# A cross-attention and graph kernel: left-out keys replaced in the context, rows transposed under the output product, reordered steps

## The chip, the cores and the metric

The kernel runs on one core of a Trainium2 chip. A core has five engines that run side by side and are tied together only by semaphores: TensorE (PE, with its weight loads as PEld), VectorE (DVE), ScalarE (ACT), GpSimd (POOL) and SyncE (SP), which here only issues DMAs. The metric is the device time of one execution in microseconds; the median over runs is compared.

## What is computed

Four layers in a row on x of shape (4, 256, 512) with a context of shape (4, 64, 512). The reference, cut to what matters:

```python
# L0: low-rank update mixed by a router
w = softmax(x @ router_W.T + router_b)
a_sum = einsum('bsh,arh->bsr', x, ctx)              # sum over the four A's
x = nan_to_num(x + 0.5 * einsum('bsn,bsnh->bsh', w, einsum('bsr,nhr->bsnh', a_sum, lora_B)))
# L1: cross-attention, 32 heads of 16, then LayerNorm
Q, K, V = x @ Wq.T + bq, ctx @ Wk.T + bk, ctx @ Wv.T + bv
attn = softmax(where(mask, Q K^T / 4, -inf)) V      # by head
x = layernorm(x + attn @ Wo.T + bo) * ln_g + ln_b
# L2 and L3, the same twice: graph of the 8 nearest, 4 blocks each
idx = the 8 nearest of 512 points, from ctx as coordinates (b, 64, 512)
for i in range(4):
    p = leaky_relu(x)
    x = (w[i] p + sum over the 8 neighbours of w[i] p) / 9 + x   # w[i] = fside[i]
```

## The kernel before

Everything runs once, batch element by batch element (b is 0 to 3), with x held transposed in four chunks of 128 features.
The order of work is written out by hand as five tables of step names, one for each engine (`PE_STEPS`, `ACT_STEPS`, `DVE_STEPS`, `POOL_STEPS`, `SP_STEPS`). A step is `kind b _ i : slot`, so `w1_2:3` is the third weights product of batch element 1, written to PSUM slot 3. There are four PSUM slots, each of 128 x 1024 fp32. Each engine walks its table strictly in order and waits on semaphores, so a step that waits holds up all that stands behind it on that engine. A slot is reused once the step that last read it is done (`wait_read` in the PE block).

The steps that matter here, by kind:

- `lora`, `router`, `mixed`, `update`: the first layer. `low` (ACT) copies the low-rank product, `rA`, `rE`, `rB` make the router's softmax and the mixture, `mh` and `ml` split it into high and low part, `raw` and `nan` (DVE) give x1.
- `dist`: distances of points, then `near` (DVE: maximum of 8 and replacement, four times for each batch element), then `adjT` on PE and `adjC` on ACT turn the marks into the adjacency matrix. `sq` (ACT) squares the coordinates as they land.
- `keys` and `values`: products of the context for all four batch elements at once. After `keys`, `kf` (ACT) adds the bias, `fm` (DVE) replaces every key that the mask leaves out by the mean of the attended keys (L989 to L999), `kh` (ACT) makes the high part, `kl` (POOL) the low part, and `kst` and `ks` (SP) carry them through HBM into `k_stack`.
- `query`: x1 times Wq in 48 matmuls; `qf`, `qh` (ACT), `ql` (POOL), then `qsh` and `qs` (SP) stack it into `q_stack`.
- `sc` and `mx`: scores for the row maximum (`shift`). `w`: the exact scores from the stacks. `ex` (ACT): the exponential. `at`: attention in 32-column tiles, with the sums of the exponentials beside it. `rc` (DVE): reciprocal of the sums. `norm`: the reciprocals are handed out to 128 rows by a product with `row_of` (L477, called from the `norm` branch). `dv`: division. `out`: product with Wo.
- `rows` (L601): x1 is transposed into a slot of its own; `ra` (ACT) copies it to `points`, `rw` (POOL) adds bo, `ad` (DVE) adds the output product and takes the statistics; `ce`, `dev`, `ln` are the LayerNorm.
- `lk`, `ph`, `pl`, `wp`, `uh`, `ul`, `sp`, `pt`: the 32 units of the graph layers (8 for each batch element). `wp` is 24 matmuls of 256 columns, `sp` is 16 of 512. `pl` on POOL makes the low part p_lo.

PE issues nearly all of its products through one helper, so L477 stands for most of them and the rows are told apart by the names of the tiles. In the rows, `slot<-xyz_n,xyz` and `slot<-points 128x512` are both `dist` (the coordinates of batch element 1 are parked in `points`), `slot<-ctx_t,wk` is `keys`, `slot<-x_hi,wq_hi` is `query`, `slot<-wv,ctx_t` is `values`.

The loads are issued by SP at the start, in this order (L377): coordinates of batch element 0, context, router weights, x of batch element 0, coordinates of 1, router bias, lora_B, Wk, mask, Wq, Wv, bv, x of 1, bo, Wo, the LayerNorm vectors, and the coordinates of 2.

## Time and profile before

| | us |
|---|---|
| median of 3 runs | 430.8 (429.2 to 431.13) |
| the profiled execution | 429.93 |
| its span, first to last instruction | 428.2 |
| PE busy | 389.0 (91% of the span) |
| DVE, ACT, POOL busy | 277.1, 156.3, 125.7 |
| mean granted clock of PE | 0.971 |

The profiled execution took 429.93 us, of which 1.7 lie outside its span; it is 0.9 below the median. The page gives sums over the whole span, then 40 slices of 10.7 us, the chain that ended last, and the costliest groups. A share of busy time is a mean over stages with different limits: the front of this kernel (the first 100 us or so) and the graph layers (from about 220 us) have to be read apart, with the timeline of each engine.

### The profile page before, as it was taken

The page shows a single profiled execution, that of the slowest core. Times are in us where ns is not written, and L with a number is a line of the kernel's source. Part 1 is how long each engine was busy: PE and PEld are TensorE (multiplying, and loading weights), DVE is VectorE, ACT ScalarE, POOL GpSimd, SP SyncE. Part 2 cuts the span into 40 slices and gives each one's busy share as a digit, 9 for nine tenths or more (in the row PEclk, how much of TensorE's full clock was granted, in tenths as well). Part 3 has the DMA queues.
Part 4 walks back from the last instruction along what each step waited for, and adds up shares of the span by engine and source line. Part 5 has one row for each costly group of instructions (what it writes and reads, how often), then busy time and mean ns, then how long its engine had stood idle before and what let it go on. Part 6 is the DMA issues. An engine that isn't in the chain of part 4 may idle for free.

```text
span 428.2 us, 5965 instructions
## 1 busy us (share of the span) xinstructions
PE 389.0 (91%) x2368; PEld 310.6 (73%) x2368; DVE 277.1 (65%) x304; ACT 156.3 (37%) x194; POOL 125.7 (29%) x78
## 2 busy tenths in 40 slices
PE   3775599869999899899999999999999999999995
PEld 1561568649659576576485998899988899888894
DVE  3824996591796767735856986567665654756543
ACT  1206405164545776233760331323323232222320
POOL 8405203220120344020324254244333341233420
PEclk9898699969999989999999999999999999999999
DMA  7980211440250353083000000000000001000012
GB/s 185 393 281 2 99 37 51 113 120 8 51 135 8 99 125 69 0 142 51 1 2 0 2 0 2 0 2 1 2 0 2 0 2 49 2 0 2 0 51 98
DMA packets 25004, 23.35 MB, mean 55 GB/s; under 512 B 8977, under 2 KB 20113, under 8 KB 24977
## 3 DMA queue, kind: packets, MB, share of 16 engines
q1 hardware_dynamic: 24528, 22.97, 19.8%
q8 instruction: 19, 0.31, 0.3%
q14 instruction: 9, 0.07, 0.1%
q10 hardware_dynamic: 448, 0.01, 0.1%
HBM read 13.26 MB, written 3.15 MB: 38 GB/s over the span
## 4 chain that ended last, share of the span: by engine, by line
PE 78%; DVE 7%; SPq 5%; ACT 4%; issue 3%; DMA 2%; ACTq 0%; DVEq 0%
PE slot L477 77%; SPq L377 5%; DMA xyz_n<-in_ctx 2%; DVE shift L1073 2%; ACT probT L805 2%; DVE k_full L989 1%; DVE near_of L981 1%; PE slot L579 1%; PE slot L587 1%; DVE top L980 1%; ACT adj L715 0%; ACT wq_hi L700 0%; DVE inv_sums L1084 0%; ACT k_full L706 0%; DVE k_part L995 0%
## 5 line engine op out<-in xcount | busy, mean ns | idle before, releaser
L894 POOL TENSOR_TENSOR p_lo<-p_full,p_hi 128x1024 fp32r<-128x1024 f32 x32 | 80.0, 2500 | 152.0 <-ACT p_hi L838 152.0
L477 PE MATMUL slot<-adj,u_hi 128*128 128x512 f32 x256 | 65.9, 399 | 0.1
L477 PE MATMUL slot<-adj,u_lo 128*128 128x512 f32 x256 | 64.8, 395 | 0.0
L1147 DVE SCALAR_TENSOR_TENSOR points<-slot,points 128x1024 f32<-128x1024 f32 x32 | 39.2, 1224 | 38.9 <-PE slot L477 38.9
L1141 DVE TENSOR_TENSOR u_lo<-slot,u_hi 128x1024 fp32r<-128x1024 f32 x32 | 39.2, 1224 | 34.4 <-ACT u_hi L847 34.4
L838 ACT ACTIVATE p_hi<-p_full 128x1024 fp32r<-128x1024 f32 x32 | 33.7, 1054 | 70.3 <-DVE p_full L1136 70.2
L847 ACT ACTIVATE u_hi<-slot 128x1024 fp32r<-128x1024 f32 x32 | 32.8, 1026 | 69.8 <-PE slot L477 69.8
L477 PEld LDWEIGHTS slot<-adj,u_lo 128*128 128x128 f32 x256 | 48.3, 188 | 11.2
L1136 DVE SCALAR_TENSOR_TENSOR p_full<-points 128x1024 f32<-128x1024 f32 x32 | 53.4, 1670 | 3.3 <-DVE points L1147 0.5
L477 PEld LDWEIGHTS slot<-adj,u_hi 128*128 128x128 f32 x256 | 47.2, 189 | 11.2 <-issue 1.0
L477 PE MATMUL slot<-fs_hi,p_hi 128*128 128x256 f32 x256 | 52.4, 286 | 0.0
L477 PE MATMUL slot<-fs_lo,p_hi 128*128 128x256 f32 x256 | 51.5, 283 | 0.0
L477 PE MATMUL slot<-fs_hi,p_lo 128*128 128x256 f32 x256 | 51.4, 282 | 0.0
L477 PEld LDWEIGHTS slot<-fs_hi,p_hi 128*128 128x128 f32 x256 | 40.7, 190 | 3.2 <-issue 1.3
L477 PEld LDWEIGHTS slot<-fs_lo,p_hi 128*128 128x128 f32 x256 | 39.7, 191 | 0.0
L477 PEld LDWEIGHTS slot<-fs_hi,p_lo 128*128 128x128 f32 x256 | 39.7, 191 | 0.0
L477 PE MATMUL slot<-wo,attT 128*128 128x512 f32 x64 | 28.2, 593 | 0.2 <-DVE attT L1088 0.2
L911 POOL TENSOR_TENSOR adj<-adj,ident 128x512 fp32r<-128x512 f32 x4 | 6.2, 1561 | 56.1 <-ACT adj L715 56.1
L477 PEld LDWEIGHTS slot<-wo,attT 128*128 128x128 f32 x64 | 12.0, 190 | 13.9 <-issue 13.4
L805 ACT ACTIVATE probT<-slot,mask_col 128x1024 f32<-128x1024 f32 x16 | 17.6, 1112 | 11.1 <-PE slot L477 11.1
L1042 DVE SCALAR_TENSOR_TENSOR x_in<-slot,x_in 128x1024 f32<-128x1024 f32 x4 | 4.9, 1222 | 23.4 <-PE slot L477 23.4
L917 POOL TENSOR_TENSOR points<-points,bo_all 128x1024 f32<-128x1024 f32 x4 | 9.5, 2376 | 34.9 <-ACT points L745 34.9
(136 smaller groups left out, 547.8 us busy)
## 6 DMA issues: line engine op xcount, KB each, us to landing
q_stack<-q_hi SPq DMA_DIRECT2D x32, 128.0 KB, 2.4
x_in<-in_xT SPq DMA_DIRECT2D x4, 512.0 KB, 5.1
q_stack<-q_lo SPq DMA_DIRECT2D x16, 128.0 KB, 3.1
out_points<-points SPq DMA_DIRECT2D x4, 512.0 KB, 2.8
loraB_raw<-in_lora_BT SPq DMA_DIRECT2D x1, 1024.0 KB, 7.9
wk<-in_WkT SPq DMA_DIRECT2D x1, 1024.0 KB, 10.1
wq_raw<-in_WqT SPq DMA_DIRECT2D x1, 1024.0 KB, 11.8
wv<-in_WvT SPq DMA_DIRECT2D x1, 1024.0 KB, 14.0
```

Of the source, the lines that this page charges most:

```text
L377: sp.dma_start(dst, src).then_inc(loads[name], 16)
L477: return pe.matmul(dst, lhsT, rhs, start=start, stop=stop, skip_group_check=True)
L805: act.activation(probT[:, i % 2, :], psum[slot_of["w", b, i]][:], ACT.Exp, bias=mask_col[:, b:b + 1], scale=QK_SCALE).then_inc(prob_ready, 1)
L838: act.activation(p_hi[b][:], p_full[:, nth["lk", b, i] % 2, :], ACT.Copy).then_inc(p_hi_ready, 1)
L847: act.activation(u_hi[:, n % 2].rearrange("p m o -> p (m o)"), psum[slot_of["wp", b, i]][:], ACT.Copy).then_inc(u_hi_ready, 1)
L894: pool.tensor_tensor(lo, full, hi.bitcast(F32), ALU.subtract).then_inc(ready, 1)
L911: pool.tensor_tensor(own, own.bitcast(F32), ident[:].unsqueeze(1).broadcast_to([P, KC, P]), ALU.add)\
L917: pool.tensor_tensor(pts, pts, bo_all[:].unsqueeze(1).broadcast_to([P, ST, H]), ALU.add)\
L1073: dve.tensor_reduce(pairs, psum[slot_of["sc", b, i]][:].rearrange("p (j a v) -> p j a v", a=2, v=V), AX_X, ALU.max, negate=True).then_inc( ...
L1136: dve.scalar_tensor_tensor(p_full[:, n % 2, :], pts, SLOPE, pts, ALU.mult, ALU.max)\
L1141: dve.tensor_tensor(u_lo[:, n % 2].rearrange("p m o -> p (m o)"), psum[slot_of["wp", b, i]][:], u_hi[:, n % 2].rearrange("p m o -> p (m o) ...
L1147: dve.scalar_tensor_tensor(pts, psum[slot_of["sp", b, i]][:], 1.0 / (TOPK + 1), pts, ALU.mult, ALU.add).then_inc(points_ready, 1)
```

## The change

- **Left-out keys.** The replacement is made before the product with Wk: `fm` masks the context into `ctx_m`, takes the mean of the attended context vectors and copies it over the left-out ones. `keys` then reads `ctx_m`. `kf` is gone; `kh` makes the high part straight from PSUM with the bias; `kl` moves from POOL to DVE and reads PSUM.
- **Rows under the output product.** `xb` (ACT) adds bo to x1 while it is still transposed and writes `x_bo`; `rows` transposes that into the slot in which `out` then accumulates. `ra`, `rw` and the addition in `ad` are gone; `st` takes the statistics, and `ce` its input, from PSUM. The slot is held from `rows` to `ce`.
- **Sums by two row tiles.** The order of heads inside `w` and `at` is rotated so that the sums of one feature chunk lie in one block of partitions. `norm` then contracts over 64 partitions instead of 128, the four products alternate between the upper and the lower half of the array, and two that follow each other write different PSUM banks.
- **Smaller edits.** The router's maximum is subtracted inside the exponential (one DVE operation fewer), the weights are normalized in the product that makes the mixture, `qh` reads PSUM instead of the SBUF copy, POOL's subtractions are cut in two or four pieces, and three of POOL's clears become steps of its table.
- **Orders.** All five tables are written anew, and so is the order of the loads: context, x of 0, mask, coordinates of 0, lora_B, Wk, coordinates of 1, x of 1, the bias columns, Wq, bo as a column (4 bytes for each descriptor), Wv, bv, the mask's columns, Wo, the LayerNorm vectors, the coordinates of 2. Router weights and bias go through ACT's queue.

The diff, cut to its core (of each table only the first line):

```diff
--- before.py
+++ after.py
...
 PE_STEPS = """
-dist0_0:0 lora0:1 dist0_1:2 router0:3 adjT0:1 keys:0 mixed0:2 lora1:3 dist1_0:1 router1:0 dist1_1:3 update0:2
...
+lora0:0 dist0_0:1 router0:2 dist0_1:3 keys:0 lora1:1 mixed0:3 values:2 router1:0 update0:1 adjT0:3 mixed1:2
...
     slot_of = {step[:3]: step[3][0] for step in pe_steps if step[3]}
+    slot_of.update({("out", b, 0): slot_of["rows", b, 0] for b in range(B)})
...
+            load(ctx_t[:], chunks(ctxT), "ctxT")
+            load_x(0)
+            load(mask_all_i[:], mask.rearrange("b v -> (b v)").unsqueeze(0).broadcast_to([P, B * V]), "mask_all")
             load_xyz(0)
-            load(ctx_t[:], chunks(ctxT), "ctxT")
-            load(a_router[:, :, R:R + NE], chunks(router_WT), "routerW")
-            load_x(0)
-            load_xyz(1)
-            load(rb_all[:], router_b.unsqueeze(0).broadcast_to([P, NE]), "rb")
             load(loraB_raw[:], chunks(lora_BT), "loraB")
             load(wk[:], chunks(WkT), "wk")
-            load(mask_all_i[:], mask.rearrange("b v -> (b v)").unsqueeze(0).broadcast_to([P, B * V]), "mask_all")
+            load_xyz(1)
+            load_x(1)
+            load(bk_col[:], bk_cols, "bk")
+            load(bq_col[:], bq_cols, "bq")
             load(wq_raw[:], chunks(WqT), "wq")
+            sp.dma_start(bo_col[:], bo.rearrange("(c p) -> p c", p=P), allow_slow_non_contiguous=True)\
+                .then_inc(loads["bo_col"], 16)
             load(wv[:], chunks(WvT), "wv")
             load(bv_all, bv.unsqueeze(0).broadcast_to([P, H]), "bv")
-            load_x(1)
-            load(bo_all[:], bo.unsqueeze(0).broadcast_to([P, H]), "bo")
+            for half in range(2):
...
+                load(mask_col_i[half * V:(half + 1) * V, :], maskT, "mask_col")
...
-                    loaded(pe, "ctxT")
+                    pe.wait_ge(ctx_filled, 1)
                     for c in range(KC):
                         for k in range(KC):
-                            last = mm(ps[:, c * B * V:(c + 1) * B * V], wk[:, k, c * P:(c + 1) * P], ctx_t[:, k, :],
+                            last = mm(ps[:, c * B * V:(c + 1) * B * V], wk[:, k, c * P:(c + 1) * P], ctx_m[:, k, :],
...
-                    after(pe, x1_ready, "nan", b)
+                    pe.wait_ge(idents, 1)
+                    after(pe, x_bo_ready, "xb", b, each=KC)
                     for t in range(ST):
                         for k in range(KC):
-                            last = pe.transpose(ps[:, t * H + k * P:t * H + (k + 1) * P],
-                                                x1[:, k, t * P:(t + 1) * P], ident[:])
-                    last.then_inc(rows_done, 1)
+                            pe.matmul(ps[:, t * H + k * P:t * H + (k + 1) * P], x_bo[b][:, k, t * P:(t + 1) * P],
+                                      ident[:], start=k == 0, stop=False, is_transpose=True, skip_group_check=True)
...
-                        pair = 4 * i + j
+                        pair = 4 * ((j + i) % KC) + j
...
-                        mm(ps[PART * j:PART * (j + 1), i * S:(i + 1) * S], v_blk[:, 4 * i + j, :],
+                        c = (j + i) % KC
+                        mm(ps[PART * j:PART * (j + 1), c * S:(c + 1) * S], v_blk[:, 4 * c + j, :],
                            probT[:, i % 2, j * S:(j + 1) * S], True, True)
                     for j in range(4):
-                        last = mm(sums[PART * j:PART * (j + 1), 0:S], sum_cols[:, i, :],
+                        c = (j + i) % KC
+                        last = mm(sums[PART * c:PART * (c + 1), 0:S], sum_cols[:, j, :],
                                   probT[:, i % 2, j * S:(j + 1) * S], i == 0, i == KC - 1)
                     last.then_inc(attend_done, 1)
                 elif kind == "norm":
-                    pe.wait_ge(blk_consts, 3)
+                    pe.wait_ge(rows_set, 1)
                     after(pe, inv_ready, "rc", b)
-                    for c in range(KC):
-                        last = mm(ps[:, c * S:(c + 1) * S], row_of[:, c, :], inv_sums[:], True, True)
+                    for c in (0, 2, 1, 3):
+                        rows = slice(2 * PART * (c // 2), 2 * PART * (c // 2 + 1))
+                        last = mm(ps[:, c * S:(c + 1) * S], row_of[rows, c % 2, :], inv_sums[rows, :], True, True)
...
-                                      k == 0, k == KC - 1)
+                                      False, k == KC - 1)
...
-                elif kind == "kf":
+                elif kind == "kh":
                     loaded(act, "bk")
                     act.wait_ge(keys_done, 1)
                     ps = psum[slot_of["keys", 0, 0]]
                     for c in range(KC):
-                        act.activation(k_full[:, c, :], ps[:, c * B * V:(c + 1) * B * V], ACT.Identity,
-                                       bias=bk_col[:, c:c + 1]).then_inc(k_ready, 1)
-                elif kind == "kh":
-                    act.wait_ge(k_filled, 1)
-                    act.activation(kT_hi[:], k_full[:], ACT.Copy).then_inc(k_hi_ready, 1)
+                        act.activation(kT_hi[:, c, :], ps[:, c * B * V:(c + 1) * B * V], ACT.Identity,
+                                       bias=bk_col[:, c:c + 1]).then_inc(k_hi_ready, 1)
...
-                elif kind == "ra":
-                    after(act, rows_done, "rows", b)
+                elif kind == "xb":
+
+                    loaded(act, "bo_col")
+                    after(act, x1_ready, "nan", b)
                     if b == 1:
-                        act.wait_ge(k_stored, 32)
+                        after(act, dist_done, "dist", 1, 1)
                     if b == 2:
                         act.wait_ge(v_ready, 1)
-                    act.activation(points[:, b].rearrange("p t n -> p (t n)"), psum[slot_of["rows", b, 0]][:],
-                                   ACT.Copy).then_inc(row_copied, 1)
+                    for c in range(KC):
+                        act.activation(x_bo[b][:, c], x1[:, c, :], ACT.Identity, bias=bo_col[:, c:c + 1])\
+                           .then_inc(x_bo_ready, 1)
...
-            def low_part(lo, full, hi, ready):
-                pool.tensor_tensor(lo, full, hi.bitcast(F32), ALU.subtract).then_inc(ready, 1)
+            def low_part(lo, full, hi, parts, ready):
+
+                n = lo.shape[1] // parts
+                for k in range(parts):
+                    cut = slice(k * n, (k + 1) * n)
+                    pool.tensor_tensor(lo[:, cut], full[:, cut], hi[:, cut].bitcast(F32), ALU.subtract)\
+                        .then_inc(ready, 1)
...
+                    link(dve.tensor_tensor(ctx_m[:], ctx_t[:],
                                            attended[:].unsqueeze(1).broadcast_to([P, KC, B * V]), ALU.mult))
-                    link(dve.tensor_reduce(k_sum[:], k_full[:].rearrange("p c (b v) -> p c b v", b=B), AX_X, ALU.add))
-                    link(dve.tensor_tensor(k_mean[:], k_sum[:], per_count[:].unsqueeze(1).broadcast_to([P, KC, B]),
+                    link(dve.tensor_reduce(ctx_sum[:], ctx_m[:].rearrange("p c (b v) -> p c b v", b=B), AX_X, ALU.add))
+                    link(dve.tensor_tensor(ctx_mean[:], ctx_sum[:], per_count[:].unsqueeze(1).broadcast_to([P, KC, B]),
                                            ALU.mult))
+                    dve.copy_predicated(ctx_m[:].rearrange("p c (b v) -> p c b v", b=B),
+                                        left_out[:].bitcast(U32).rearrange("p (b v) -> p b v", b=B).unsqueeze(1)
+                                        .broadcast_to([P, KC, B, V]),
+                                        ctx_mean[:].unsqueeze(3).broadcast_to([P, KC, B, V])).then_inc(ctx_filled, 1)
+                elif kind == "kl":
+                    dve.wait_ge(ctx_filled, 1)
+                    ps = psum[slot_of["keys", 0, 0]]
                     for c in range(KC):
-                        last = dve.tensor_tensor(k_part[:, c].rearrange("p (b v) -> p b v", b=B),
-                                                 left_out[:].rearrange("p (b v) -> p b v", b=B),
-                                                 k_mean[:, c].unsqueeze(2).broadcast_to([P, B, V]), ALU.mult)
-                    link(last)
-                    dve.tensor_tensor(k_full[:], k_full[:], k_part[:], ALU.add).then_inc(k_filled, 1)
+                        dve.wait_ge(k_hi_ready, 2 * (c // 2 + 1))
+                        dve.scalar_tensor_tensor(kT_lo[:, c, :], ps[:, c * B * V:(c + 1) * B * V], bk_col[:, c:c + 1],
+                                                 kT_hi[:, c, :].bitcast(F32), ALU.add, ALU.subtract)\
+                           .then_inc(k_lo_ready, 1)
...
-                elif kind == "ad":
-                    after(dve, row_ready, "rw", b)
-                    ps = psum[slot_of["out", b, 0]]
+                elif kind == "st":
+                    ps = psum[slot_of["rows", b, 0]]
                     for t in range(ST):
                         after(dve, half_output if t == 0 else output_done, "out", b)
-                        pts = points[:, b, t]
-                        dve.tensor_tensor(pts, pts, ps[:, t * H:(t + 1) * H], ALU.add).then_inc(sum_ready, 1)
-                        dve.wait_ge(sum_ready, ST * nth["ad", b, 0] + t + 1)
-                        link(dve.bn_stats(stats[:, b, t], pts))
...
+                        link(dve.bn_stats(stats[:, b, t], ps[:, t * H:(t + 1) * H]))
...
-                        dve.scalar_tensor_tensor(points[:, b, t], points[:, b, t], mean_var[:, b, t, 0:1], g_all[:],
-                                                 ALU.subtract, ALU.mult).then_inc(centered, 1)
+                        dve.scalar_tensor_tensor(points[:, b, t], ps[:, t * H:(t + 1) * H], mean_var[:, b, t, 0:1],
+                                                 g_all[:], ALU.subtract, ALU.mult).then_inc(centered, 1)
```

How the orders move. TensorE at the start, before:

```order
L477 MATMUL slot<-xyz_n,xyz 128x512 x2
L477 MATMUL slot<-x_in,points 72x256 x4
L477 MATMUL slot<-xyz_n,xyz 128x512 x2
L561 MATMUL slot<-ident,low 128x72 x2
L579 MATMUL slot<-ident_h,near_of 128x128 x16
L477 MATMUL slot<-ctx_t,wk 128x256 x16
L587 MATMUL slot<-ident,mix 128x128 x8
L477 MATMUL slot<-x_in,points 72x256 x4
L477 MATMUL slot<-points 128x512 x2
L561 MATMUL slot<-ident,low 128x72 x2
L477 MATMUL slot<-points 128x512 x2
```

and with the change (`slot<-ctx_m,wk` is `keys`):

```order
L480 MATMUL slot<-x_in,points 72x256 x4
L480 MATMUL slot<-xyz_n,xyz 128x512 x2
L566 MATMUL slot<-ident,low 128x72 x2
L480 MATMUL slot<-xyz_n,xyz 128x512 x2
L480 MATMUL slot<-ctx_m,wk 128x256 x16
L480 MATMUL slot<-x_in,points 72x256 x4
L592 MATMUL slot<-ident,mix 128x128 x8
L480 MATMUL slot<-wv,ctx_t 128x512 x8
L566 MATMUL slot<-ident,low 128x72 x2
L480 MATMUL slot<-mixT_hi,loraB_hi 128x256 x4
L480 MATMUL slot<-mixT_hi,loraB_lo 128x256 x4
L480 MATMUL slot<-mixT_lo,loraB_hi 128x256 x4
```

`lora` of batch element 0 now opens; `keys`, the second `lora` and `values` stand ahead of the first `adjT` (the 16 transposes of `near_of`) and of both `dist` products of batch element 1.

ScalarE at the start, before (`xyz_n<-xyz_n` is `sq` of batch element 2, `adj<-slot` is `adjC`):

```order
L697 ACTIVATE loraB_hi<-loraB_raw 128x2048
L726 ACTIVATE lge<-lgs 128x16
L694 ACTIVATE xyz_n<-xyz_n 64x512
L715 ACTIVATE adj<-slot,taken_bias 128x2048
L700 ACTIVATE wq_hi<-wq_raw 128x2048
L706 ACTIVATE k_full<-slot,bk_col 128x256 x4
L732 ACTIVATE mixT_hi<-slot 128x1024
L723 ACTIVATE low<-slot 72x256
L710 ACTIVATE kT_hi<-k_full 128x1024
```

and with the change (`points<-points` is `sq` of batch element 1):

```order
L703 ACTIVATE loraB_hi<-loraB_raw 128x2048
L730 ACTIVATE lge<-lg,small 128x8 x2
L700 ACTIVATE points<-points 64x512
L706 ACTIVATE wq_hi<-wq_raw 128x2048
L712 ACTIVATE kT_hi<-slot,bk_col 128x256 x4
L788 ACTIVATE k_blk_hi<-kT_hi,half_col 32x4x64 x8
L736 ACTIVATE mixT_hi<-slot 128x1024
L726 ACTIVATE low<-slot 72x256
L700 ACTIVATE xyz_n<-xyz_n 64x512
```

`sq` of batch element 2 stood ahead of `adjC`, `mh` and the second `low`, and stands behind `kh`, `kb`, `mh` and that `low` now.

VectorE around the keys, before:

```order
L987 RECIPROCAL per_count<-count 128x4
L989 TENSOR_TENSOR k_full<-k_full,attended 128x1024
L991 TENSOR_REDUCE k_sum<-k_full 128x16
L992 TENSOR_TENSOR k_mean<-k_sum,per_count 128x16
L995 TENSOR_TENSOR k_part<-left_out,k_mean 128x256 x4
L999 TENSOR_TENSOR k_full<-k_full,k_part 128x1024
L1037 TENSOR_TENSOR mixT_lo<-slot,mixT_hi 128x1024
```

and with the change, first the part ahead of the product, then the part behind it:

```order
L1010 TENSOR_TENSOR ctx_m<-ctx_t,attended 128x1024
L1012 TENSOR_REDUCE ctx_sum<-ctx_m 128x16
L1013 TENSOR_TENSOR ctx_mean<-ctx_sum,per_count 128x16
L1015 COPY_PREDICATED ctx_m<-left_out,ctx_mean 128x1024
L1046 TENSOR_TENSOR lg<-slot,rb_all 128x16
```

and

```order
L1054 SCALAR_TENSOR_TENSOR mix<-slot,small,lge 128x512 x2
L984 TENSOR_SCALAR mask_col<-mask_col_i 128x4
L1024 SCALAR_TENSOR_TENSOR kT_lo<-slot,bk_col,kT_hi 128x256 x4
L1060 TENSOR_TENSOR mixT_lo<-slot,mixT_hi 128x1024
L1030 TENSOR_TENSOR v_rows<-slot,points 128x1024
```

The mask arithmetic of eight operations that stood between the product and the first `ml` is now ahead of the product and of the first router step; behind the product four operations on a quarter of the columns each are left.

## Rows read from the trace of the kernel before

**Rows 1.** The page: busy time of the engines, and GB/s in 40 slices of 10.7 us.
```profile
PE 389.0 (91%) x2368; PEld 310.6 (73%) x2368; DVE 277.1 (65%) x304; ACT 156.3 (37%) x194; POOL 125.7 (29%) x78
...
GB/s 185 393 281 2 99 37 51 113 120 8 51 135 8 99 125 69 0 142 51 1 2 0 2 0 2 0 2 1 2 0 2 0 2 49 2 0 2 0 51 98
```

**Rows 2.** Waits of PE over the whole span: total us, times, longest.
```profile
PE slot L477 <- ACT xyz_n L694: 6.4, 1, 6.4
PE slot L477 <- DVE mixT_lo L1037: 6.1, 1, 6.1
PE slot L477 <- ACT adj L715: 5.5, 1, 5.5
PE slot L477 <- ACT probT L805: 4.1, 8, 1.5
PE slot L477 <- DVE shift L1073: 3.7, 1, 3.7
PE slot L579 <- DVE near_of L981: 2.9, 1, 2.9
...
PE slot L561 <- ACT low L723: 1.1, 1, 1.1
```

**Rows 3.** Windows: length, then busy us of PE, PEld, DVE, ACT, POOL, then clock, DMA share, GB/s.
```profile
0.00:63.90 63.90, 41.52 (x181) 27.90 (x182) 41.56 (x68) 17.27 (x26) 21.66 (x35) 0.89 0.52 167
63.90:100.00 36.10, 29.74 (x184) 24.08 (x182) 26.12 (x38) 16.20 (x27) 8.93 (x4) 0.91 0.32 86
100.00:230.00 130.00, 124.00 (x863) 88.75 (x862) 87.58 (x105) 66.55 (x86) 29.22 (x12) 0.99 0.27 56
230.00:428.20 198.20, 193.71 (x1147) 169.81 (x1145) 121.86 (x95) 56.28 (x56) 65.86 (x27) 1.00 0.03 11
```

**Rows 4.** Timeline of ACT: start us, us, line, operation, [idle before, releaser].
```profile
32.28 0.63 ACT L694 ACTIVATE xyz_n<-xyz_n 64x512 f32<-64x512 f32 x1 [10.56 <-DMA xyz_n<-in_ctx]
...
38.02 1.05 ACT L732 ACTIVATE mixT_hi<-slot 128x1024 fp32r<-128x1024 f32 x1
...
47.76 3.69 ACT L775 ACTIVATE k_blk_hi<-kT_hi,half_col 32x256 fp32r<-32x256 f32 x8
```

**Rows 5.** Timeline of DVE, same columns: the masking of the keys begins and ends.
```profile
38.26 4.11 DVE L989 TENSOR_TENSOR k_full<-k_full,attended 128x1024 f32<-128x1024 f32 x1 [13.34 <-ACT k_full L706]
42.40 1.22 DVE L991 TENSOR_REDUCE k_sum<-k_full 128x16 f32<-128x1024 f32 x1
...
46.47 1.22 DVE L1037 TENSOR_TENSOR mixT_lo<-slot,mixT_hi 128x1024 fp32r<-128x1024 f32 x1
```

**Rows 6.** Timeline of PE: keys, two distance steps, and the first rows step.
```profile
18.70 8.12 PE L477 MATMUL slot<-ctx_t,wk 128*128 128x256 f32 x32
...
34.95 3.37 PE L477 MATMUL slot<-points 128*128 128x512 f32 x4 [5.53 <-ACT adj L715]
...
39.69 1.96 PE L477 MATMUL slot<-points 128*128 128x512 f32 x4
...
63.86 1.04 PE L601 MATMUL slot<-ident,x 128*128 128x128 f32 x8
```

**Rows 7.** Timeline of PE: two products in 32-column tiles, then the full-array norm product.
```profile
109.57 0.64 PE L477 MATMUL slot<-probT,v_blk 128*32 128x256 f32 x8
110.03 0.61 PE L477 MATMUL slot<-probT,sum_cols 128*32 128x256 f32 x8
...
118.22 1.97 PE L477 MATMUL slot<-inv_sums,row_of 128*128 128x256 f32 x8
```

**Rows 8.** Timeline of POOL where DVE shows a long operation.
```profile
36.77 4.51 POOL L894 TENSOR_TENSOR wq_lo<-wq_raw,wq_hi 128x2048 fp32r<-128x2048 f32 x1 [0.53 <-ACT wq_hi L700]
```

**Rows 9.** DMA issues by line: KB each, median us from issue to landing.
```profile
x_in<-in_xT SPq DMA_DIRECT2D x4, 512.0 KB, 5.1
...
ctx_t<-in_ctxT SPq DMA_DIRECT2D x1, 512.0 KB, 4.4
```

**Rows 10.** Timeline of SyncE: the stack reload of the third batch element begins.
```profile
151.49 5.67 SPq L411 DMA_DIRECT2D q_stack<-q_hi  x8
```

281 lines of the change are left out of this document (143 added, 138 removed).

## The prediction, made before the change was run

> **What bounds the kernel now.** I read the page's busy times first, then what PE waits for, then the span in four windows, then the timelines of the front. PE is busy 389.0 of 428.2 us [rows 1], so at most 39.2 us of idle time are there to win besides faster work. The windows say where they lie [rows 3]. From 230 us to the end PE is busy 193.7 of 198.2 us at full clock, and the missing 4.5 us are the last update of the points and the last store, which nothing in the change shortens. From 100 to 230 us it is idle 6.0 us, mostly in eight short waits for the exponential [rows 2, 3]. From 63.9 to 100 us it is idle 6.4 us, of which 3.7 are a wait for the row maxima on DVE [rows 2, 3]. The first 63.9 us hold the rest: PE is busy 41.5 us there and idle 22.4 us, and its granted clock is 0.89 on average [rows 3]. So the graph layers are bound by PE, and the front by what PE waits for.
>
> The timelines name the chain of the front. ACT walks its table in order, and the square of the third coordinate set stood waiting 10.6 us for its load, until 32.3 us [rows 4]. Behind it stood the adjacency copy (5.5 us of PE's waits) and the high part of the first mixture, at 38.0 us [rows 2, 4]. Then DVE spent 38.3 to 46.5 us on the masked keys before it came to the low part of that mixture, for which PE waited 6.1 us [rows 2, 5]. The first of those mask operations took 4.11 us, where the next one of the same width took 1.22; it ended at 42.37, and POOL's subtraction beside it ended at 36.77 + 4.51 = 41.28 [rows 5, 8]. The other waits before 63.9 us are 6.4 us for the first coordinates, 2.9 for the neighbours and 1.1 for the low-rank copy [rows 2].
>
> **Term 1, the front's waits.** I follow the new order with durations of the rows.
>
> - Start. The context is now issued first and x second, at about 0.8 and 1.4 us by the issue times of the old first loads. With 4.4 and 5.1 us to landing [rows 9] they are there at 5.2 and 6.5, and the sum over the context on DVE needs 1.3 us behind the first. I let the first product start at 7.5, against 6.4 before: 1.1 us lost.
> - Keys. The product needs Wk and the masked context. Through Wk 3.5 MB are issued; at 185 GB/s in the first 10.7 us and 393 GB/s after it [rows 1] that is 2.0 MB and then 1.5 MB in 3.9 us, so 14.6 us. The mask chain took 46.47 - 38.26 = 8.2 us [rows 5]. Without the hold-up beside POOL (4.11 - 1.22 = 2.9) and with one predicated copy in place of five operations (a gain of about 1.3) it is 4.0. It starts behind about 2.6 us of small operations from 6.5 on, so it ends at 13.1, or at 15 if POOL's clears hold it up once. Keys start near 15 instead of 18.7 [rows 6]. PE has two distance steps, a router and a low-rank product to do till then, and hardly waits.
> - From there PE has the second low-rank product, the mixture, values and a router step, some 10 us of work behind the 7 of keys, so until 32. The first low part of the mixture needs the new ACT chain: keys end at 22, then 1.6 for the high part, 3.7 for the block of keys (it took 3.69 [rows 4]), 1.05 and 1.22 for the two parts of the mixture [rows 4, 5]: 29.6. So it comes 2.4 us ahead of its use, and the 6.1 us wait is gone. The square of the third coordinates still waits to about 32 us, but what stands behind it is wanted later than that. The 5.5 us and the 1.1 us waits go too.
>
> What is late next is the second mixture's low part, behind the first x1 on DVE: I get about 1 us of wait. PE's idle time in this stage falls from 22.4 to 7.5 + 0.5 to 1, say 8.0: **14.4 us won**. At best 15.4, with no later wait; at worst 10, if keys start no earlier than at 18.7 as before.
>
> **Term 2, the clock of the front.** At a clock of 0.89 over 63.9 us, 11% is lost, which is 14 us at the half level of 1.2 GHz. About half of it lies under idle time. A distance step at 34.95 us took 3.37 us, just behind the 5.5 us wait, and the next 1.96 [rows 6]; keys took 8.12 us. Without the long waits most of this goes; the first steps at the very start stay slow. I take **4.5 us**, with 0 and 7 as ends.
>
> **Term 3, the sums handed out by two row tiles.** One norm step takes 1.97 us [rows 7]. The trace of before has no row tiles, but it has column tiles: four 256-column products in four 32-column tiles start at 109.57, and the next four at 110.03, so 0.46 us for four, against 1.97 for four on the full array [rows 7]. Two tiles at a time should take half: 0.98. Four steps win 4 x 0.98 = 3.9; at worst nothing, if the halves run one after the other. I take **3.8**.
>
> The page on tiling (the Trainium skill, TensorEngine Tiling, section Tiling Modes) says that a change of the tiling mode drains the array. By it each norm step would pay for two changes of mode and give part of the 3.8 us back. The trace shows no such price: the 32-column products at 109.57 and 110.03 follow each other and their neighbours without a gap beyond 0.1 us [rows 7], so the sum keeps its term.
>
> **Terms at nothing.** POOL loses four additions of bo and the low part of the keys, DVE the additions of the output product and some router steps. They are hidden beside PE already, where DVE is busy 87.6 of 130 us [rows 3]; if the waits in the middle were theirs, a gain of up to 6 us, and I count none. ACT gains work: the biased copy is four operations instead of one, and the order puts a square root between two exponentials once more, so two table loads come in. Beside 66.5 busy us of 130 [rows 3] ACT has room; each load could delay one exponential, 2.6 us at worst. The slot of the transposes is held longer at the front by 1 us of PE, and at the back the DVE work until it is free is about equal. The stack reloads of SP take 12 to 13 us from the last weights product of one batch element (it began at 151.5 for the third [rows 10]). In the new order some 16 us of PE work lie between, so they just fit. Splitting POOL's subtractions of the graph layers lets DVE in earlier, and PE never waits there [rows 3]: nothing.
>
> The middle from 63.9 to 230 us I leave at its 12.4 us of idle time: by the same walk the new order still waits some 3.5 us for the row maxima and 3 for the second-next mixture, and some 5 us in pieces behind that. Ends: 6 us either way.
>
> **The sum.** 14.4 + 4.5 + 3.8 = 22.7 off the profiled 429.9 gives 407.2. That execution lies 0.9 below the median of 430.8, so **408** for the median. As a cross-check from below: 389.0 - 3.8 - 4.5 busy, + 8.0 + 12.4 + 4.5 idle, + 1.7 outside the span = 407.3. With all ends good it is 430.8 - 15.4 - 7 - 3.9 - 6 = 398.5, with all bad 430.8 - 10 - 0 - 0 + 6 + 2.6 = 429.4, and both are unlikely.
>
> **The rivals.**
>
> - *The middle tightens too.* DVE is busy 41.6 and 26.1 us in the first two windows, more than anything but PE [rows 3], and it loses work there. If the waits of the middle fall from 12.4 to about 4 us, the time is 399. For it: the waits for row maxima and neighbours are DVE's [rows 2]. Against it: the five DVE operations that make x1 between update and query stay as they are. 0.13.
> - *A load is late in the new order.* The square of the third coordinates still stands in ACT's table with the load the last in a queue of about 8 MB; bo comes as 512 pieces of 4 bytes ahead of Wv. Each us beyond 35 puts off the next router step, and with it the first x1. At 43 instead of 32 us it costs 8: 416. For it: the first 32 us are at the full rate of the DMA engines already [rows 1]. Against it: the queue carries 0.25 MB less. 0.12.
> - *The clock does not rise in the front.* With a start of short products and waits strewn between, PE could stay at 1.2 GHz until 44 us. That is 36 us of full-speed work at half speed, less 2 that I counted: 34 more, 442, **slower** than before. It decides from the point at which 22 us of that work run at the half level. Against it: before, it rose in the first 20 us in spite of waits of 2.9 us, and the window's mean is 0.89 [rows 3]. 0.03.
> - *The front is not what holds the end.* If PE, once ahead, waits in the middle for something with a time of its own (the stack reloads, the LayerNorm chain into the graph layers), the lead goes and about 430 is left. Against it: none of the 6 us between 100 and 230 is a wait for a DMA [rows 2]. 0.02.
>
> **How the numbers follow.** The forecast has 0.70, with a range of its own of 402 to 414. Leaving out the two worst rivals and the outer part of the others gives 397 to 419 for 8 in 10. About 0.5% is what a measurement of this kernel can tell from no change. Faster by more than that holds the forecast and the first two rivals: 0.95; within it the last: 0.02; slower the clock: 0.03.
>
> **What would show it.** Right: PE's first product near 7.5 us, keys near 15, the first update near 32 instead of 47.8, PE idle about 8 us before the point at which both values and the distances of batch element 1 are done (near 44 us); norm steps near 1.0 us; 198 us of graph layers as before. Wrong: a norm step of 1.97, a first update behind 38 us, new waits of PE in the middle above 12 us, or idle time of PE in the graph layers.

## The result, and the profile after

The changed kernel takes 420.2 us (median of 4 runs, 418.9 to 421.0) against 430.5 for the kernel before in the same comparison: a ratio of 0.977, with a 95% interval of 0.975 to 0.979. It is faster by 10.3 us, where 23 were forecast: 408 with a range of 397 to 419, so it lies 1.2 us above the range. The profiled execution took 421.0 us, of which 419.3 are its span. Some executions of a version run a per cent or more longer at a lower clock, and the medians and ranges below hold them while the ratios leave them out: one of four with a whole p_lo (420.3; the other three have a median of 414.8) and two of ten with the old load order (434.1 and the profiled 435.3; the other eight have 430.4).

The busy times on the page of the changed kernel, against [rows 1]:

```profile
PE 382.8 (91%) x2368; PEld 307.2 (73%) x2368; DVE 247.3 (59%) x288; ACT 163.7 (39%) x223; POOL 125.9 (30%) x115
```

PE's busy time fell by 6.2 us and its idle time from 39.2 to 36.5 only. The windows, columns as in [rows 3], with their first window cut in two at 44 us, where the values and the distances of batch element 1 are done:

```profile
0.00:44.00 44.00, 35.79 (x164) 23.85 (x164) 27.99 (x53) 18.30 (x29) 20.67 (x40) 1.00 0.78 237
44.00:63.90 19.90, 16.94 (x122) 16.31 (x121) 10.68 (x17) 4.97 (x12) 0.00 (x0) 0.83 0.09 27
63.90:100.00 36.10, 28.87 (x214) 21.54 (x211) 26.84 (x38) 20.56 (x37) 6.30 (x5) 0.91 0.33 82
100.00:230.00 130.00, 119.88 (x791) 85.08 (x791) 82.10 (x102) 67.23 (x95) 22.49 (x18) 0.99 0.30 53
230.00:419.30 189.30, 181.27 (x1087) 160.45 (x1085) 99.69 (x81) 52.63 (x52) 76.42 (x52) 1.00 0.03 12
```

Length minus PE's busy time gives the idle time: 8.2, 3.0, 7.2, 10.1 and 8.0 us. Before, the first 63.9 us held 22.4, then 6.4, 6.0 and 4.5 [rows 3]. So 11.2 us of waits went from the front, and 8.4 came back behind it: 4.9 between 63.9 and 230 us, 3.5 in the graph layers. What PE waited for, against [rows 2]:

```profile
PE slot L480 <- DMA x_in<-in_xT: 7.2, 1, 7.2
PE slot L480 <- POOL p_lo L909: 4.1, 4, 1.2
PE slot L480 <- issue: 4.0, 2, 3.0
PE slot L622 <- DVE shift L1096: 3.8, 1, 3.8
PE slot L480 <- ACT probT L821: 3.2, 7, 1.1
PE slot L480 <- DVE shift L1096: 2.8, 4, 0.9
PE slot L584 <- issue: 2.3, 1, 2.3
PE slot L592 <- DVE mix L1054: 2.3, 1, 2.3
PE slot L480 <- DVE near_of L1002: 1.2, 1, 1.2
```

The front itself, on PE, against [rows 6] (start us, us, then the products, as there):

```profile
7.21 3.69 PE L480 MATMUL slot<-x_in,points 128*72 128x256 f32 x8 [7.21 <-DMA x_in<-in_xT]
...
16.27 7.14 PE L480 MATMUL slot<-ctx_m,wk 128*128 128x256 f32 x32 [1.00 <-issue]
...
32.81 0.72 PE L480 MATMUL slot<-mixT_hi,loraB_hi 128*128 128x256 f32 x4
...
40.44 3.60 PE L480 MATMUL slot<-points 128*128 128x512 f32 x8
46.99 1.20 PE L480 MATMUL slot<-mixT_hi,loraB_hi 128*128 128x256 f32 x4 [2.96 <-issue]
47.99 1.05 PE L480 MATMUL slot<-mixT_hi,loraB_lo 128*128 128x256 f32 x4
...
53.11 0.68 PE L480 MATMUL slot<-mixT_hi,loraB_lo 128*128 128x256 f32 x4
```

First product at 7.2 (7.5 predicted), keys at 16.3 (15), first update at 32.8 (32) instead of 47.8, distances done at 44.0 (44). Behind them stands a wait of 2.96 us where I had counted one of about 1, and after it PE runs at 1.2 GHz for 6 us (46.99 to 53.1): four 256-column products take 0.85 us, behind that 0.48. On ACT, against [rows 4], the square for the third coordinates is hardly earlier than before (31.93 against 32.28 us); what changed is what stands ahead of it:

```profile
25.71 3.69 ACT L788 ACTIVATE k_blk_hi<-kT_hi,half_col 32x256 fp32r<-32x256 f32 x8
29.43 1.02 ACT L736 ACTIVATE mixT_hi<-slot 128x1024 fp32r<-128x1024 f32 x1
...
31.93 0.63 ACT L700 ACTIVATE xyz_n<-xyz_n 64x512 f32<-64x512 f32 x1 [1.22 <-DMA xyz_n<-in_ctx]
```

On DVE the low part of the second mixture (45.68, the one that the 2.96 us wait is for) stands behind the five operations that make x1; the first one's, at 30.48, answers to the one at 46.47 of [rows 5]:

```profile
30.48 1.23 DVE L1060 TENSOR_TENSOR mixT_lo<-slot,mixT_hi 128x1024 fp32r<-128x1024 f32 x1 [2.17 <-ACT mixT_hi L736]
...
44.50 1.29 DVE L1082 COPY_PREDICATED x<-scratch,x_in 128x1024 f32<-128x1024 uint32 x1
45.68 1.21 DVE L1060 TENSOR_TENSOR mixT_lo<-slot,mixT_hi 128x1024 fp32r<-128x1024 f32 x1
```

The norm product, of which the old one took 1.97 us [rows 7]:

```profile
109.57 1.14 PE L480 MATMUL slot<-inv_sums,row_of 64*128 64x256 f32 x8
```

### The profile page after: what moved, and what is told of

Read it like the earlier page. It is cut to its first block, busy times and chain, and to the rows that moved or that the text cites. A ratio compares the mean times of both kernels' runs of the same rounds, so it can differ in the third digit from the quotient of the medians.

```text
span 419.3 us, 6016 instructions
## 1 busy us (share of the span) xinstructions
PE 382.8 (91%) x2368; PEld 307.2 (73%) x2368; DVE 247.3 (59%) x288; ACT 163.7 (39%) x223; POOL 125.9 (30%) x115
## 4 chain that ended last, share of the span: by engine, by line
PE 81%; DVE 6%; ACT 4%; issue 4%; POOL 3%; DMA 1%; SPq 0%; ACTq 0%; DVEq 0%; POOLq 0%
PE slot L480 78%; POOL p_lo L909 3%; DVE shift L1096 2%; DMA x_in<-in_xT 1%; ACT probT L821 1%; DVE points L1167 1%; ACT p_hi L861 1%; PE slot L584 1%; DVE p_full L1156 1%; PE slot L592 1%; PE slot L607 1%; ACT L821 1%; DVE mix L1054 0%; DVE top L1001 0%; ACT q_hi L766 0%
## 5 line engine op out<-in xcount | busy, mean ns | idle before, releaser
L909 POOL TENSOR_TENSOR p_lo<-p_full,p_hi 128x512 fp32r<-128x512 f32 x64 | 91.4, 1450 | 191.4 <-ACT p_hi L861 191.4
L1167 DVE SCALAR_TENSOR_TENSOR points<-slot,points 128x1024 f32<-128x1024 f32 x32 | 39.2, 1224 | 47.8 <-PE slot L480 47.7
L480 PE MATMUL slot<-adj,u_hi 128*128 128x512 f32 x256 | 64.9, 397 | 0.0
L870 ACT ACTIVATE u_hi<-slot 128x1024 fp32r<-128x1024 f32 x32 | 32.8, 1026 | 78.7 <-PE slot L480 78.7
L1156 DVE SCALAR_TENSOR_TENSOR p_full<-points 128x1024 f32<-128x1024 f32 x32 | 40.9, 1281 | 3.2 <-POOL p_lo L909 0.5
L909 POOL TENSOR_TENSOR q_lo<-q_full,q_hi 128x512 fp32r<-128x512 f32 x8 | 10.1, 1285 | 62.9 <-ACT q_full L775 41.3
L1096 DVE TENSOR_REDUCE shift<-slot 128x16 f32<-128x1024 f32 x16 | 18.9, 1215 | 9.5 <-PE slot L480 9.5
L480 PE MATMUL slot<-k_blk_hi,q_hi 128*128 128x512 f32 x32 | 11.8, 464 | 4.7 <-DVE shift L1096 2.4
## 6 DMA issues: line engine op xcount, KB each, us to landing
wk<-in_WkT SPq DMA_DIRECT2D x1, 1024.0 KB, 11.2
```

The source lines that it names most:

```text
L480: return pe.matmul(dst, lhsT, rhs, start=start, stop=stop, skip_group_check=True)
L870: act.activation(u_hi[:, n % 2].rearrange("p m o -> p (m o)"), psum[slot_of["wp", b, i]][:], ACT.Copy).then_inc(u_hi_ready, 1)
L909: pool.tensor_tensor(lo[:, cut], full[:, cut], hi[:, cut].bitcast(F32), ALU.subtract)\
L1096: dve.tensor_reduce(pairs, psum[slot_of["sc", b, i]][:].rearrange("p (j a v) -> p j a v", a=2, v=V), AX_X, ALU.max, negate=True).then_inc( ...
L1156: dve.scalar_tensor_tensor(p_full[:, n % 2, :], pts, SLOPE, pts, ALU.mult, ALU.max)\
L1167: dve.scalar_tensor_tensor(pts, psum[slot_of["sp", b, i]][:], 1.0 / (TOPK + 1), pts, ALU.mult, ALU.add).then_inc(points_ready, 1)
```

## The experiments

**Which part of the new order carries the front.** `sq2` is the square of the third coordinates. ACT_STEPS of the kernel before had it ahead of the first mixture's high part; the new table has it behind. Moved alone behind it (and behind `low1`), in the kernel before:

```diff
-sq0 sq1 low0 lbh rE0 sq2 adjC0 wqh kf mh0 low1 kh kb0 rE1 xh0 adjC1 ra0 mh1 vb0 qf0 qh0 low2 xh1 rE2 sq3 kb1 ra1 sh0
+sq0 sq1 low0 lbh rE0 adjC0 wqh kf mh0 low1 sq2 kh kb0 rE1 xh0 adjC1 ra0 mh1 vb0 qf0 qh0 low2 xh1 rE2 sq3 kb1 ra1 sh0
```

> The kernel before with one step moved in ACT's table: the square of the third coordinates, which waits for the last load until 32 us, goes behind the second low-rank copy. Theory (in-order ACT waiting for that load is what held the front): the 5.5 us wait for the adjacency goes, the high part of the first mixture is there at about 29.5 instead of 39.1 us, the masked keys on DVE begin at 28.5 instead of 38.3, and the first update begins near 38 instead of 47.8; 5 to 9 us faster in the end, 421 to 425. Rival (the front is held by the chain of the keys, or the lead is waited out in the middle): under 3 us faster.

Measured: 419.6 us (418.0 to 421.0), ratio 0.974 (0.970 to 0.979). One step moved in one table gives 10.7 us, more than the 5 to 9 expected and as much as the whole change. Its windows (as above) hold 12.9, 1.8, 5.5, 6.1 and 4.5 us of idle time:

```profile
0.00:44.00 44.00, 31.13 (x145) 21.41 (x146) 30.57 (x56) 17.08 (x25) 21.87 (x35) 1.00 0.74 235
44.00:63.90 19.90, 18.06 (x116) 13.52 (x115) 15.29 (x23) 7.33 (x11) 4.17 (x2) 1.00 0.16 44
63.90:100.00 36.10, 30.56 (x200) 25.16 (x199) 20.71 (x29) 13.72 (x24) 7.16 (x3) 0.86 0.28 72
100.00:230.00 130.00, 123.92 (x811) 85.94 (x812) 92.93 (x114) 63.45 (x82) 29.17 (x12) 0.99 0.27 56
```

Its front idles 14.7 us up to 63.9, 3.5 more than that of the change, and its middle 11.6 against 17.3. The converse, `sq2` put back ahead of `wqh` in the new table (in the version with p_lo made by one instruction, which takes 415.1 us, see below):

```diff
-sq0 low0 lbh rE0 sq1 wqh kh kb0 mh0 low1 sq2 vb0 rE1 adjC0 mh1 xb0 xh0 qh0 qf0 adjC1 low2 kb1 xh1 rE2 xb1 sh0 sq3
+sq0 low0 lbh rE0 sq1 sq2 wqh kh kb0 mh0 low1 vb0 rE1 adjC0 mh1 xb0 xh0 qh0 qf0 adjC1 low2 kb1 xh1 rE2 xb1 sh0 sq3
```

> The changed kernel with the low part of p in one instruction (415.1 us), and on ACT sq2 put back where the kernel before had it: ahead of the high parts of Wq and of the keys, the keys' rows, the first mixture's high part and low1. Theory: ACT stands at sq2 until the square for it is there, near 32 us, and all behind it with it; the first mixture's high part comes near 38 instead of 28 us, update0 starts near 41 instead of 33 us, and the kernel takes 8 to 10 us more: 423 to 425 us. Rival: the change's other moves (the context first, the orders of DVE and POOL) carry the front by themselves, and it costs under 3 us: at most 418 us.

Measured: 426.4 us (424.6 to 428.4), ratio 0.989 (0.983 to 0.995), 11.2 more than the 415.1 of the version it was made from (8 to 10 expected). In its timeline ACT stands again, and PE behind it; this is the old wait in the new kernel, first on ACT and then on PE:

```profile
31.84 0.63 ACT L700 ACTIVATE xyz_n<-xyz_n 64x512 f32<-64x512 f32 x1 [13.61 <-DMA xyz_n<-in_ctx]
...
39.67 1.02 ACT L736 ACTIVATE mixT_hi<-slot 128x1024 fp32r<-128x1024 f32 x1
40.59 0.37 ACT L726 ACTIVATE low<-slot 72x256 f32<-72x256 f32 x1
...
41.11 0.47 PE L566 MATMUL slot<-ident,low 72*128 72x72 f32 x2 [8.68 <-ACT low L726]
```

PE began its first update at 42.1 us (41 expected). Both directions agree. The windows of this run behind the front answer a further question, whether the lead of the front is what PE waits out in the middle:

```profile
63.90:100.00 36.10, 29.29 (x196) 24.86 (x195) 22.39 (x35) 16.71 (x37) 3.74 (x3) 0.91 0.29 72
100.00:230.00 130.00, 119.28 (x843) 83.18 (x842) 82.03 (x99) 69.71 (x98) 23.00 (x14) 1.00 0.31 56
```

Here the front is late by 10 us, and the middle still idles 6.8 + 10.7 = 17.5 us. The old order has 12.4 with a late front and 11.6 with an early one, the new order 17.5 with a late front and 17.3 with an early one (17.0 with a whole p_lo). So these waits of the middle come with the order and not with the lead.

**The subtraction of p in two instructions.** Undone in the changed kernel:

```diff
-                    low_part(p_lo[b][:], p_full[:, nth["lk", b, i] % 2, :], p_hi[b][:], 2, p_lo_ready)
+                    low_part(p_lo[b][:], p_full[:, nth["lk", b, i] % 2, :], p_hi[b][:], 1, p_lo_ready)
```

> The changed kernel with the low part p_lo of the graph layers made in one POOL operation again, as before; nothing else altered. Theory A (the split lets DVE's p_full operation in between the two halves, which puts off the second half by 1.1 us and makes TensorE wait: four waits, 4.1 us in all): the four waits for p_lo vanish, p_full on DVE goes from a mean of 1281 ns back to about 1670 ns, and the time is 4 us under the changed kernel's 420.2, so about 416. Rival (the graph layers are bound by TensorE and the waits would only come up elsewhere, or the split lets the next unit begin earlier): 420, within 1 us.

Measured: 415.1 us (413.9 to 420.3), ratio 0.968 (0.960 to 0.975), 5 us less. Idle time behind 230 us is back at 4.6 us, and PE's waits for p_lo fall from 4.1 to 0.5. POOL and DVE at one place of the graph layers, first the changed kernel:

```profile
386.91 3.55 POOL L909 TENSOR_TENSOR p_lo<-p_full,p_hi 128x512 fp32r<-128x512 f32 x2 [7.07 <-ACT p_hi L861]
...
388.12 1.23 DVE L1156 SCALAR_TENSOR_TENSOR p_full<-points 128x1024 f32<-128x1024 f32 x1
```

and then with one instruction:

```profile
381.38 2.40 POOL L909 TENSOR_TENSOR p_lo<-p_full,p_hi 128x1024 fp32r<-128x1024 f32 x1 [6.11 <-ACT p_hi L861]
...
382.58 2.28 DVE L1156 SCALAR_TENSOR_TENSOR p_full<-points 128x1024 f32<-128x1024 f32 x1
```

With one, POOL ends in 2.40 us and DVE's `p_full` takes 2.28, ending 1.08 behind POOL. With two, DVE comes in between the halves, takes 1.23, and POOL's pair takes 3.55; PE, which waits for POOL's second half, then stands 1.23 us. Over the whole kernel `p_lo` costs POOL 91.4 instead of 76.6 us and `p_full` on average 1281 instead of 1607 ns. The Trainium skill (SBUF — State Buffer, section Who interferes with whom) says that a DVE instruction with two SBUF inputs and a GpSimd instruction that reads SBUF contend for a port pair that is locked, and that the order of issue decides who is blocked. Both timelines agree: the one that began second ended about its own time behind the end of the first. A shorter instruction gives the port away sooner, here to the operation that had time.

The same edit in the kernel before:

> The kernel before with only p_lo split in two halves. Theory A: p_full falls from 1670 to about 1280 ns, p_lo takes longer as a pair, and TensorE, which never waited in the graph layers, now waits for POOL where p_lo is wanted soon after p_full: 2 to 5 us slower than 430.5. Rival (only the new orders have p_lo that late): no difference, 430.5 within 1 us.

Measured: 434.5 us (433.8 to 436.5), ratio 1.010 (1.006 to 1.013), 4 us more, with three new waits for p_lo of 3.3 us together. The cost does not depend on the new order.

**The row tiles alone.** In the kernel before, the sums laid out for two tiles of 64 rows, all else as it was (cut to the `norm` step; the heads are rotated as in the change):

```diff
-                        last = mm(ps[:, c * S:(c + 1) * S], row_of[:, c, :], inv_sums[:], True, True)
+                        rows = slice(2 * PART * (c // 2), 2 * PART * (c // 2 + 1))
+                        last = mm(ps[:, c * S:(c + 1) * S], row_of[rows, c % 2, :], inv_sums[rows, :], True, True)
```

> The kernel before with only the sums handed out by two row tiles (the rotation of heads, the sums by block, and the norm product over 64 partitions in the order 0, 2, 1, 3). Theory: each norm step falls from 1.97 to 1.14 us as in the changed kernel, all four stand where TensorE has other work right behind, so 4 x 0.83 = 3.3 us faster: about 427.2. Rival (norm is followed by a wait on DVE's division or on an exponential, so the time saved is waited out): at most 1 us faster.

Measured: 429.1 us (10 runs, 428.6 to 432.1), ratio 0.997 (0.994 to 0.999): 1.2 us, nearer to the rival than to the 3.3 of the theory. The group of these products in the kernel before (busy us, mean ns of one | idle time before it):

```profile
L477 PE MATMUL slot<-inv_sums,row_of 128*128 128x256 f32 x32 | 7.7, 384 | 0.1
```

The same group with the row tiles:

```profile
L477 PE MATMUL slot<-inv_sums,row_of 64*128 64x256 f32 x32 | 4.5, 401 | 0.0
```

So 3.2 us of PE's time go, 0.8 for each step, and 2 of them don't show in the end. About 1 us is found in two waits a step or two behind a norm step, where the trace of the kernel before shows none; where the rest goes stays open:

```profile
119.15 1.14 PE L477 MATMUL slot<-inv_sums,row_of 64*128 64x256 f32 x8
...
121.27 1.09 PE L601 MATMUL slot<-ident,x 128*128 128x128 f32 x8 [0.70 <-DVE shift L1078]
...
183.92 1.13 PE L477 MATMUL slot<-inv_sums,row_of 64*128 64x256 f32 x8
...
186.49 0.47 PE L477 MATMUL slot<-fs_hi,p_hi 128*128 128x256 f32 x2 [0.44 <-POOL p_lo L899]
```

Whether it is the change of half from product to product that pays was asked by handing out the products in the order 0, 1, 2, 3:

```diff
-                    for c in (0, 2, 1, 3):
+                    for c in range(KC):
```

> The changed kernel with the four products of a sum handed out in the order 0, 1, 2, 3 instead of 0, 2, 1, 3, so that two products in a row stand on the same half of the rows and two on the same half of the columns. Theory: the norm step took 1.14 instead of 1.97 us because neighbouring products stand on different halves of the array and overlap; in this order the overlap is partly lost and the step takes 1.5 to 2.0 us. Rival: what counts is the smaller product alone, in any order, and the step stays at 1.1 to 1.2 us. The total can move by at most 4 x 0.8 us = 3 us, and hardly shows it.

Measured: 419.0 us in one run, and all four steps take 1.14 us, as in the changed kernel: the order makes no difference, and the theory, which had 1.5 to 2.0 us, fails. The step is shorter in either order, and why it takes 1.14 and not 0.98 us stays open.

**The two small edits together**, in the kernel before:

> The kernel before with the two single edits of e3 and e4 together: row tiles for the sums, and the square of the third coordinates moved behind the second low-rank copy on ACT. If the two add: 430.3 - 10.7 - 1.2 = 418.4, which is below the whole change's 420.2. If the row tiles only help where the front is late: 419.6, as e4.

Measured: 418.0 us (417.7 to 418.1), ratio 0.969 (0.965 to 0.973): the two add, as expected. Two edits of a few lines beat the whole change (420.2) by 2 us. Once p_lo is whole (415.1), the rest of the change adds 2.9 us by the medians and next to nothing by the ratios to the kernel before in the same comparison (0.969 and 0.968). Of that rest one part was tried on top: the low parts of lora_B and of Wq made in four pieces.

```diff
-                    low_part(wq_lo[:], wq_raw[:], wq_hi[:], wq_lo_ready)
+                    for k in range(KC):
+                        low_part(wq_lo[:, k], wq_raw[:, k], wq_hi[:, k], wq_lo_ready)
```

> The kernel before with sq2 behind low1, the row tiles for the sums, and one thing more of the change: the low parts of lora_B's and Wq's rows made by POOL in four pieces instead of one instruction each. Against the version without the pieces (418.0 us). Theory: one long POOL subtraction holds back DVE's operations beside it until it ends (in the kernel before k_full took 4.11 us beside the low part of Wq, which took 4.51); in pieces DVE comes in between, lgs and k_full take 1 to 2 us each, and what follows the keys starts earlier: 414 to 416 us. Rival: DVE's time there is not what the first updates wait for any more, and the time stays at 417 to 419 us.

Measured: 416.5 us (413.2 to 418.2), ratio 0.968 (0.961 to 0.974). By time alone it can't be told from the version without the pieces; the timelines can. Without the pieces, DVE shows long operations:

```profile
17.07 4.50 DVE L1030 TENSOR_TENSOR lgs<-lg,small 128x16 f32<-128x16 f32 x1
...
28.35 2.80 DVE L994 TENSOR_TENSOR k_full<-k_full,attended 128x1024 f32<-128x1024 f32 x1 [2.38 <-ACT k_full L709]
```

and POOL, at the time of the first of them:

```profile
17.03 4.51 POOL L899 TENSOR_TENSOR loraB_lo<-loraB_raw,loraB_hi 128x2048 fp32r<-128x2048 f32 x1 [5.48 <-ACT loraB_hi L700]
```

With the pieces, the same two operations of DVE:

```profile
17.21 1.14 DVE L1032 TENSOR_TENSOR lgs<-lg,small 128x16 f32<-128x16 f32 x1
...
26.83 1.27 DVE L996 TENSOR_TENSOR k_full<-k_full,attended 128x1024 f32<-128x1024 f32 x1 [2.72 <-ACT k_full L709]
```

An operation of 16 columns took 4.50 us because it began 0.04 us behind a POOL instruction of 4.51 us, and 1.14 behind a piece; with no POOL instruction beside it it takes 0.17. The first update then starts at 33.5 instead of 36.6 us. Here nobody needs POOL's product soon, and splitting brings the front forward, though the whole time does not show it clear of noise; in the graph layers PE waits for it at once, and it costs.

**The order of the loads.** The changed kernel with the load order of before:

```diff
+            load_xyz(0)
             load(ctx_t[:], chunks(ctxT), "ctxT")
             load_x(0)
-            load(mask_all_i[:], mask.rearrange("b v -> (b v)").unsqueeze(0).broadcast_to([P, B * V]), "mask_all")
-            load_xyz(0)
+            load_xyz(1)
             load(loraB_raw[:], chunks(lora_BT), "loraB")
             load(wk[:], chunks(WkT), "wk")
-            load_xyz(1)
-            load_x(1)
+            load(mask_all_i[:], mask.rearrange("b v -> (b v)").unsqueeze(0).broadcast_to([P, B * V]), "mask_all")
             load(bk_col[:], bk_cols, "bk")
...
             load(wq_raw[:], chunks(WqT), "wq")
-            sp.dma_start(bo_col[:], bo.rearrange("(c p) -> p c", p=P), allow_slow_non_contiguous=True)\
-                .then_inc(loads["bo_col"], 16)
             load(wv[:], chunks(WvT), "wv")
             load(bv_all, bv.unsqueeze(0).broadcast_to([P, H]), "bv")
+            load_x(1)
+            sp.dma_start(bo_col[:], bo.rearrange("(c p) -> p c", p=P), allow_slow_non_contiguous=True)\
+                .then_inc(loads["bo_col"], 16)
             for half in range(2):
```

> The changed kernel with its loads issued by SyncE in the order of before (coordinates first, the mask behind Wk, x of batch element 1 behind bv), router weights and bias still through ACT. Theory (the order of the loads is worth what it moves the masked context and Wk): the mask lands near 18 us instead of 8, so the masked context is ready near 23 instead of 13.7 and keys start near 23 instead of 16.3; everything behind shifts by 5 to 7 us, about 426. Rival (the front has slack there and the in-order ACT with its wait for the last load decides): within 2 us of 420.2.

Measured: 432.0 us (10 runs, 427.3 to 435.3), ratio 0.998 (0.993 to 1.003), 10 to 12 more, where 6 were expected. The mask lands late on DVE, and keys wait for the masked context:

```profile
10.51 3.69 PE L480 MATMUL slot<-x_in,points 128*72 128x256 f32 x8 [10.51 <-DMA x_in<-in_xT]
...
18.03 1.40 DVE L1006 TENSOR_SCALAR attended<-mask_all_i 128x256 f32<-128x256 int32 x1 [9.10 <-DMA mask_all_i<-in_mask]
...
25.84 9.82 PE L480 MATMUL slot<-ctx_m,wk 128*128 128x256 f32 x32 [7.96 <-DVE ctx_m L1015]
```

The masked context needs the mask, and in the old order the mask stands behind lora_B and Wk. So the new computation needs the mask early, which the new load order gives; with it the first product starts earlier too, at 7.2 instead of 10.5 us. What each of the moved loads is worth by itself was not tried.

**The clock.** In the version with a whole p_lo, 22 products that nobody reads fill the wait ahead of the second update:

> The kernel of e1 (p_lo whole), with 22 products that nobody reads issued on TensorE in the 3.0 us wait before the second update, into the slot that this update is about to overwrite. Theory (that wait lets TensorE fall to 1.2 GHz, and seven of the twelve groups of the update then start 0.85 us apart instead of 0.48): the update runs at full speed, 2.7 us are won, 412.5 against the 415.1 of e1, and the granted clock of 44 to 64 us rises to 1.00. Rival (the next product waits for x_lo on VectorE anyway, which is ready near 50 us, or the time is waited out before the row maxima): 415, within 1 us.

Measured: 415.3 us (414.3 to 416.1), no gain. The clock from 44 to 63.9 us rose from 0.91 to 1.00, but a bf16 step behind a later wait ran in 1.86 us where it takes 1.05 at full speed. The filling need not be the cause: the same step ran as slowly in the profiled execution of the version with the order 0, 1, 2, 3, which fills nothing. First with the filling, then without any:

```profile
110.66 1.86 PE L589 MATMUL slot<-ident_h,near_of 128*128 128x128 bf16 x16 [2.33 <-issue]
...
110.14 1.87 PE L584 MATMUL slot<-ident_h,near_of 128*128 128x128 bf16 x16 [2.33 <-issue]
```

With all four long waits filled (before `shift0`, `mixed2` and `adjT2` too):

```diff
+                if (kind, b) == ("shift", 0):
+                    keep_warm(psum[2][:, 2 * S:3 * S], 30)
```

> As e5, with products that nobody reads in three more waits of TensorE: 30 before shift0 (3.8 us wait), 16 before the third mixture (2.3 us), 18 before the third adjacency transposes (2.3 us), each into a part of a slot that nobody holds. Theory: the steps behind these waits (mixture 1.9 instead of 1.0 us, the first two groups of the second query, the w1, sc2 and update3 products around 120 us) run at full speed, another 2 to 3 us: 409 to 411. Rival (what stands behind these waits is followed by further waits, which take up the gain): like e5.

Measured: 414.0 us (411.2 to 415.5), ratio 0.959 (0.953 to 0.964), the lowest median of all, where 409 to 411 was the theory. Its profiled execution, the one of 411.2 us, has a clock of 0.999, and the group behind the old 2.96 us wait runs at full speed from the start. The other three executions have 0.987 or 0.988, hardly more than the 0.983 to 0.986 of the fast ones with a whole p_lo, and take as long as those. So a gain by filling the waits is not shown beyond one execution.

**The table loads.** Two steps put so that ACT changes its table twice less, again in the version with a whole p_lo:

```diff
-ex3_0 dev2 ex3_1 ex3_2 ph0_2 ex3_3 ph2_0 ac3 uh0_2 uh1_0 ph0_3 dev3 uh0_3 ph3_0 uh2_0 ph1_1 uh3_0 ph0_4 uh1_1 ph2_1
+ex3_0 ex3_1 ex3_2 ph0_2 ex3_3 dev2 ph2_0 ac3 uh0_2 uh1_0 ph0_3 dev3 uh0_3 ph3_0 uh2_0 ph1_1 uh3_0 ph0_4 uh1_1 ph2_1
...
-ul0_0 sl3 pt0_0 lk0_1 rc2 st1 dv2 ce1 ln1 ul0_1 lk1_0 st2 ce2 pt0_1 ln2 lk0_2 lk2_0 rc3 dv3 ul0_2 ul1_0 pt0_2 lk0_3
+ul0_0 sl3 pt0_0 lk0_1 rc2 st1 dv2 ce1 ln1 ul0_1 lk1_0 st2 ce2 pt0_1 lk0_2 ln2 lk2_0 rc3 dv3 ul0_2 ul1_0 pt0_2 lk0_3
```

> The changed kernel with the low part of p in one instruction (415.1 us), and two ACT steps put so that ACT changes its function table twice less (two loads of 1.28 us each). Theory: part of these 2.6 us is on the path of the graph layers' powers: 412.5 to 414.5 us. Rival: both loads lie beside ACT's idle time and the time stays at 414.5 to 416 us.

Measured: 418.7 us (416.5 to 419.6), ratio 0.971 (0.965 to 0.977), 3.6 more by the medians: neither theory. `dev2` now runs at 204.6 instead of 192.8 us; behind it on ACT a `ph` waits 3.1 us for DVE, `attT` behind that runs at 209.0, and the timeline of PE has a wait that it had not:

```profile
210.06 1.13 PE L480 MATMUL slot<-inv_sums,row_of 64*128 64x256 f32 x8 [1.92 <-ACT attT L831]
```

That is 1.9 us. In this profiled execution keys also waited 1.78 instead of 0.44 us and the bf16 step shown above took 1.86 us, both long before the steps that moved, so the edit explains about half of the 3.6. Two loads saved (8 before, 6 now) were worth less than the place of the steps; what a load itself costs was not isolated.

## Why the prediction was wrong

The sum had 380.7 us busy and 24.9 idle. Measured in the profiled execution: 382.8 and 36.5. Of the 13.7 us between them 11.6 are idle time.

- **The middle, left at its 12.4 us of idle time.** This step failed, together with the next one. Between 63.9 and 230 us PE idles 17.3 us (17.0 with a whole p_lo): +4.9. The walk had the first two waits right (3.5 for the row maxima: 3.8; 3 for the mixture: 2.3), and behind them 5 us in pieces; there stand 11.2: 2.3 before `adjT2`, 2.8 for `shift` in four waits, 3.2 for the exponential, 1.2 for the neighbours, 0.7 for the stack, 0.6 for p_lo, 0.4 for a mixture. In the kernel with only `sq2` moved the middle keeps 11.6, and in the new order with `sq2` put back, without any lead, it has 17.5. So it isn't the lead that is waited out; the new order has these waits itself. Which of its moves makes each was not tried and stays open. My own bound for "new waits of PE in the middle above 12 us" was the right alarm.
- **Splitting POOL's subtractions at nothing.** The premise, that PE never waits there, was true of before [rows 3] and false for what the split makes of it: 5 us by the undone split, 4 us by the split alone in the kernel before. I had used the hold-up of DVE beside POOL in term 1 ([rows 5, 8]) and did not turn it round: if DVE comes in, POOL is late, and PE waits for POOL. Counted at 5, it would have made the forecast 413, and with 4.9 more for the middle 418.
- **Term 1, the front: 11.2 of 14.4 us.** Up to 44 us 8.2 us idle, as forecast (8.0), each start within 1.3 us. Missed is the later wait, 2.96 instead of about 1 us: the second mixture's low part stands behind the whole of x1 on DVE, whose last operation ends at 45.8 us. The mechanism was the right one, and one part of the change carries it: `sq2` alone 10.7 us, and back 11.2.
- **Term 2, the clock: about 3 of 4.5 us.** PE's busy time fell by 6.2 us, 3.2 of it the norm steps. The first 44 us do run at 1.00, but the new wait before the second update and those at 74 and 77 us slow what stands behind them (windows at 0.83 and 0.91).
- **Term 3, the row tiles: 3.2 of 3.8 us of PE's time, 1.2 of the end.** A step takes 1.14, not 0.98 us; alone 1.2 us show, and on top of the moved step 1.6. The estimate rested on two halves that run side by side, and no run shows that: the step takes the same when neighbouring products share a half. The cost of a change of tiling mode, weighed there, is not to be seen as a gap here either: around the row above (183.92) the 32-column groups before and behind it start at 183.34 and 184.98, so they follow at once. If there is one inside the 1.14 us, no run tells it apart.
- **Terms at nothing, the rest.** Two more table loads did come in (8 against 6), of 1.28 us each; the one edit that saved two cost more through the steps it moved, so no run shows their own price. The stack reload fits but for 0.7 us.
- **The rivals.** None came as written. The middle grew instead of tightening; no load was late (`sq2` at 31.93); the clock rose. Nor did the lead go in the middle, as the last one has it: the idle time there is the same with the lead and without it.

The gain that was there is larger than the change's: 430.3 to 415.1 us with a whole p_lo alone.

## What to carry to other kernels

In an order written out by hand, look first for the one step that waits at the head of an in-order engine's table for data that come late, and move that step alone: it may be worth as much as reordering everything. Splitting an instruction on GpSimd is a decision on who gets the port that it shares with VectorE: it helps where VectorE's operation is wanted first (a first update 3.1 us earlier here), and costs where TensorE waits for GpSimd's result (4 to 5 us). A walk of a new order must be carried through to the end of the stage in which engines wait for each other; idle time of the old order is no estimate for the new one.

## What the runs showed of the hardware

- A VectorE operation with two SBUF inputs of 16 columns took 4.50 us beside a GpSimd subtraction that began 0.04 us before it, against 0.17 with no GpSimd instruction beside it. The blocked operation ended with the blocker (17.07 + 4.50 and 17.03 + 4.51).
- Four products over 64 rows instead of 128, two on each half of the array, take a norm step from 1.97 to 1.14 us, whether neighbouring products change the half or not.
- The clock behind a 2.33 us wait differs between executions: the same bf16 step took 1.05 us in some and 1.86 in others, filled waits or not. Filling one wait left the time where it was (415.3 against 415.1), filling four gave 0.999 in one execution and 0.987 or 0.988 in three.
- A function table load took 1.28 us each time, and ACT's next instruction began at once behind it. Taking two of them off made TensorE wait 1.9 us for the steps that moved with them.
